# A preparation stage written as a straight plan: biases inside the products, rows normalised on ScalarE, rows of x loaded ahead of the weights, and results handed over by halves in the expert stage

## The chip, the cores and the metric

The kernel runs on one core of a Trainium2 chip. The core has five engines with their own instruction lists: TensorE (PE: products and transposes into PSUM), VectorE (DVE), ScalarE (ACT: functions from tables), GpSimd (POOL) and SyncE (SP), which here only issues DMAs. They run side by side and meet at semaphores. The metric is the time of one execution on the device in microseconds (us).

## The reference

The input x is (8, 1024, 256): 8 batches of 1024 rows of 256 channels. It goes through five blocks, each added to x: causal attention with 16 heads, a mixture of 8 experts (each row goes to one expert, at most 512 rows an expert), an RWKV-7 block, and the same mixture again. The change lies mostly in what is computed ahead of the recurrence of the RWKV-7 block. With xn the normalised rows:

```
shifted = rows of xn moved down by one, first row zero;  delta = shifted - xn
xr, xw, xk, xv, xa = xn + delta * x_r, x_w, x_k, x_v, x_a
r = xr @ W_r;  k = xk @ W_k;  v = xv @ W_v
log_w = -softplus(-(tanh(xw @ w_lora_a) @ w_lora_b + w_lora_bias)) - 0.5
a = sigmoid(xa @ a_lora_a @ a_lora_b + a_lora_bias)
g = sigmoid(r @ g_lora_a) @ g_lora_b + g_lora_bias
kk = k * k_k, scaled to norm 1 in each head;  k = k * (1 + (a - 1) * k_a)
o = recurrence over (r, log_w, k, v, -kk, kk * a);  bonus = ((r * k * r_k).sum(head)) * v
```

An expert computes `gelu(rows @ wi) @ wo`, scaled by the row's weight and added to the row.

## The kernel before, in words

Six stages follow one another with a barrier between: `attention`, `mixture`, `prepare`, `recurrence`, `finish`, `mixture`. The change touches `prepare` and the second half of `mixture`.

`prepare` works on one batch of 1024 rows a turn; all tensors lie in 8 tiles of 128 rows by 256 channels, or turned as 2 x 128 channels by 1024 rows. What is done in a turn, and in which order, stands in a list of jobs, `prepare_turn`, of stages with a half or a letter. Every engine goes through the same list and does its own part of each job, so an engine's instructions stand in the list's order, and each waits by semaphore for what it needs. A job marked `+` belongs to the next batch. The stages:

- `normalise` (L1997): VectorE makes mean and variance of each row (`bn_stats`, `bn_aggr`), ScalarE the root, VectorE the reciprocal and `xn`. `turn_x` (L1877, L1936): TensorE transposes `xn`, ScalarE copies it to `turned`.
- `mix` (L1979): VectorE makes `delta` (with the mix of r) and then the mixed rows of one letter, two instructions of 128x1024. v uses w's buffer, k uses a's.
- `r`, `k`, `v` (L1882): products with the full weights. ScalarE copies r to `r_rows`; `turn_r` transposes r (L1889).
- `w_inner`, `a_inner`, `g_inner` (L1896): the inner products with 64, 64 and 128 columns, then tanh, copy or sigmoid on ScalarE. `w`, `a`, `g` (L1909): the outer products. For w and a VectorE adds the bias into `z_w`, `z_a` (L2029), and ScalarE takes the sigmoid in place (L1957, L1960). For g VectorE adds the bias into `gate_sb` (L2034).
- `v` on ScalarE (L1940): three copies each half, into the packed rows that the recurrence reads.
- `key` (L2036): a chain on VectorE with two short steps on ScalarE, for each half of k. `bonus` (L2062): two VectorE instructions a half. GpSimd multiplies r by r_k and by k beside it (L1847, L1853).

Each product goes into one of four PSUM slots, handed out in the list's order; TensorE waits until the slot's last reader has emptied it. The turns of batches 0 to 6 are a hardware loop (`Fori`, L1770), the last turn is written out. Ahead of the first turn stands `prepare_start`. SyncE issues 20 loads of weights, then x of batches 0 and 1 (L1793, L1824); TensorE and VectorE wait for all of the weights at their start.

In the expert half of `mixture` (L1110 to L1273) TensorE makes the four tiles of an expert's result (`ps_res`, two PSUM banks) in one run and signals at its end; VectorE adds all four (L1221), signals, and GpSimd scatters four times (L1181).

## Time and profile before

| | us |
|---|---|
| median of three runs (lowest, highest) | 4567.62 (4563.92, 4568.98) |
| the profiled execution | 4533.91 |
| its span | 4532.2 |
| TensorE, VectorE, ScalarE, GpSimd busy | 3957.9, 3275.1, 1467.1, 2043.5 |
| mean granted TensorE clock | 0.929 |

The profile describes one execution. Times of rows count from the span's start. A row of a timeline has the start, the time busy, the engine, the line of the kernel, the operation, what is written and read, and the count of like instructions merged; in brackets stands how long the engine had stood idle before and which instruction ended the wait. PEclk and clock are the clock that TensorE was granted, as a share of 2.4 GHz, so 0.50 is 1.2 GHz. A float32 product is listed as two passes, so 16 products have a count of 32. Merged rows overlap their neighbours by a little; spacing is read from start to start.

### The profile page before, as it was taken

Reading aid. Unit: us, or ns where it says so; the run is one execution under the profiler, and the core shown is the slowest. Engines: PE = TensorE matmul, PEld = TensorE weight load, DVE = VectorE, ACT = ScalarE, POOL = GpSimd, SP = SyncE. Lnnn points to the kernel's source line nnn. Section 1 sums busy time; section 2 is a strip of 40 time slices with the busy share of each in tenths; the row PEclk is TensorE's granted clock in tenths of the full one; section 3 lists DMA queues with packets and bytes.
Section 4 is the critical chain, followed back from the end, with each engine's and each line's share of the span. In section 5 each row is a group of like instructions: output and inputs, shape, how many; then the busy total and the mean of one; then the engine's idle time right before and its main releaser. Section 6 shows DMA issues by size and latency. Waiting matters only on the chain. (4 is left out here: it accounts for less than half of the span.)

```text
span 4532.2 us, 66896 instructions
## 1 busy us (share of the span) xinstructions
PE 3957.9 (87%) x23448; PEld 2705.1 (60%) x23448; DVE 3275.1 (72%) x8604; ACT 1467.1 (32%) x2404; POOL 2043.5 (45%) x1669
## 2 busy tenths in 40 slices
PE   5999999999986895888669999999999999555698
PEld 2344444444436563666558888888888888444565
DVE  5777777877746002898769999999999999686410
ACT  2666666666665111444301111111111111013411
POOL 2211211221125221111168888888888888421522
PEclk7999999999996897999889999999999999776699
DMA  4322332332337231344443232323232322365432
GB/s 109 84 76 76 85 85 67 88 88 66 84 86 222 85 129 47 137 162 150 161 80 41 34 42 33 42 34 42 34 42 35 40 37 32 85 213 172 153 126 78
DMA packets 495631, 394.81 MB, mean 87 GB/s; under 512 B 298635, under 2 KB 457638, under 8 KB 489185
## 3 DMA queue, kind: packets, MB, share of 16 engines
q1 hardware_dynamic: 483040, 365.68, 32.8%
q0 software_dynamic: 12288, 25.28, 1.7%
q8 instruction: 168, 2.75, 0.3%
q14 instruction: 135, 1.10, 0.1%
HBM read 230.52 MB, written 167.97 MB: 88 GB/s over the span
## 5 line engine op out<-in xcount | busy, mean ns | idle before, releaser
L749 DVE TENSOR_REDUCE at_neg_max<-at_slot 128x1 f32<-128x512 f32 (+3 forms) x1216 | 745.8, 655 | 247.9 <-PE at_slot L541 245.1
L671 ACT ACTIVATE at_prob<-at_slot 128x512 f32<-128x512 f32 (+1 forms) x1216 | 631.1, 577 | 354.4 <-PE at_slot L561 353.5
L1613 PE MATMUL sc_added<-sc_outer,sc_ident 128*128 128x128 f32 x4096 | 586.4, 287 | 72.3 <-POOL sc_outer L1449 56.9
L1580 ACT ACTIVATE sc_seen<-sc_state 128x512 f32<-128x512 f32 x256 | 152.8, 597 | 1479.2 <-DVE sc_decayed L1529 1455.8
L1613 PEld LDWEIGHTS sc_added<-sc_outer,sc_ident 128*128 128x128 f32 x4096 | 496.9, 192 | 202.7 <-DVE sc_state L1561 109.8
L1462 POOL TENSOR_TENSOR sc_terms<-sc_seen,sc_pack 128x1024 f32<-128x1024 f32 (+2 forms) x288 | 604.9, 2142 | 13.8 <-PE sc_ps_o L1635 13.8
L1635 PE MATMUL sc_ps_o<-sc_terms,sc_ident 128*128 128x256 f32 x2048 | 607.6, 381 | 2.1 <-POOL sc_terms L1462 2.1
L389 POOL TENSOR_SCALAR_AFFINE_SELECT at_prob<-at_prob 128x512 f32<-128x512 f32 x256 | 162.8, 636 | 887.4 <-ACT at_prob L671 887.2
L541 PE MATMUL at_slot<-at_k_stack,at_q_stack 96*128 96x512 bf16 (+3 forms) x1536 | 458.7, 334 | 24.4 <-DMA at_k_stack<-parts 22.0
L1449 POOL TENSOR_TENSOR sc_outer<-sc_pack 128x2048 f32<-128x2048 f32 x128 | 467.2, 3672 | 5.0
L561 PE MATMUL at_slot<-at_q_stack,at_k_stack 99*128 99x512 bf16 (+3 forms) x1536 | 453.3, 331 | 12.1 <-ACT at_prob L671 11.7
L1525 DVE TENSOR_TENSOR sc_prod<-sc_state,sc_pack 128x256 f32<-128x256 f32 x1024 | 387.0, 424 | 3.7 <-POOL sc_from_v L1442 3.7
L1534 DVE TENSOR_REDUCE sc_u<-sc_prod 128x16 f32<-128x256 f32 x1024 | 386.5, 424 | 0.0
L1619 PE MATMUL sc_added<-sc_decayed,sc_ident 128*128 128x128 f32 x2048 | 365.1, 301 | 10.3 <-DVE sc_decayed L1529 1.0
L578 PE MATMUL at_values<-at_prob,at_v_rows 128*32 128x512 f32 (+3 forms) x3072 | 333.7, 505 | 16.2 <-POOL at_prob L389 16.2
L561 PEld LDWEIGHTS at_slot<-at_q_stack,at_k_stack 99*128 99x128 bf16 x1536 | 140.3, 97 | 325.9 <-issue 252.8
L1619 PEld LDWEIGHTS sc_added<-sc_decayed,sc_ident 128*128 128x128 f32 x2048 | 267.5, 190 | 103.3 <-DVE sc_decayed L1529 101.8
L1561 DVE TENSOR_TENSOR sc_state<-sc_added,sc_rank 128x128 f32<-128x128 f32 x1024 | 255.1, 295 | 92.8 <-PE sc_added L1624 65.5
L1635 PEld LDWEIGHTS sc_ps_o<-sc_terms,sc_ident 128*128 128x128 f32 x2048 | 313.5, 192 | 4.0 <-POOL sc_terms L1462 2.5
L1624 PE MATMUL sc_added<-sc_rank,sc_ident 128*128 128x128 f32 x2048 | 313.6, 276 | 2.2
L1624 PEld LDWEIGHTS sc_added<-sc_rank,sc_ident 128*128 128x128 f32 x2048 | 275.7, 191 | 55.1 <-DVE sc_rank L1539 5.1
L1539 DVE TENSOR_TENSOR sc_rank<-sc_u,sc_pack 128x128 f32<-128x128 f32 x1024 | 245.4, 281 | 0.0
(244 smaller groups left out, 6185.6 us busy)
## 6 DMA issues: line engine op xcount, KB each, us to landing
packed<-pr_pack SPq DMA_DIRECT2D x16, 3072.0 KB, 13.4
sc_pack<-packed SPq DMA_DIRECT2D x512, 96.0 KB, 3.6
parts<-at_parts SPq DMA_DIRECT2D x96, 256.0 KB
f_up_w<-in_ffn_wi SPq DMA_DIRECT2D x16, 1024.0 KB, 5.0
f_down_w<-in_ffn_wo SPq DMA_DIRECT2D x16, 1024.0 KB, 8.3
at_q_stack<-parts SPq DMA_DIRECT2D x32, 384.0 KB
at_k_stack<-parts SPq DMA_DIRECT2D x32, 384.0 KB
slots<-at_no_row SPq DMA_DIRECT2D x2, 4128.0 KB, 21.3
```

The source lines that it names most:

```text
L541: last = pe.matmul(by_head[:, j, :], q_stack[0:6 * D, h + j, qt * P:(qt + 1) * P], k_stack[0:6 * D, h + j, k0:k0 + tiles * P], start=not d ...
L561: last = pe.matmul(by_head[:, j, :], k_stack[0:6 * D + 3, h + j, kt * P:(kt + 1) * P], q_stack[0:6 * D + 3, h + j, q0:q1], start=True, sto ...
L671: act.activation(prob[:, first:first + n, q1 - tiles * P:q1], ps[:, 0:n * tiles * P].rearrange("p (n k) -> p n k", n=n), ACT.Exp)\
L749: dve.tensor_reduce(neg_max[:, chunk, qt, h:h + n], ps[:, 0:n * tiles * P].rearrange("p (n k) -> p n k", n=n), AX.X, ALU.max, negate=True) ...
L1449: own.up(pool.tensor_tensor(outer[m % 2][:, t, :].rearrange("p t (i j) -> p t i j", j=D), pack[m % 4][:, t, FV * D:(FV + 1) * D].unsqueeze ...
L1462: return pool.tensor_tensor(terms[m % 2][:].rearrange("p (n s) (j i) -> p n s i j", s=2, j=D)[:, pair:pair + n, step], seen[:, slot:slot + ...
L1525: dve.tensor_tensor(prod[:, h * STATE:(h + 1) * STATE].rearrange("p (s i j) -> p s i j", s=2, j=D), old[:, rows[h], :].unsqueeze(1).broadc ...
L1534: dve.tensor_reduce(u[:, pair, :, rows[h]], prod[:, h * STATE:(h + 1) * STATE].rearrange("p (s i j) -> p s i j", s=2, j=D), AX.X, ALU.add) ...
L1613: pe.matmul(added[h][:, 0:HALF], ident[:], outer[m % 2][:, 2 * n + s, h * HALF:(h + 1) * HALF], start=(s == 0), stop=False)
L1619: pe.matmul(added[h][:, 0:HALF], ident[:], decayed[:, h * HALF:(h + 1) * HALF], start=False, stop=False)
L1624: pe.matmul(added[h][:, 0:HALF], ident[:], rank[:, 0, h * HALF:(h + 1) * HALF], start=False, stop=True)\
L1635: last = pe.matmul(ps_o[m % 2][:], ident[:], by_column[:, n], start=first, stop=last_one)
```

## The change

In the list of a turn, `w_inner` stands ahead of `turn_r`; `normalise` is split into `stats` and `affine`, which stand behind `a` and around the mix of k, where `normalise` stood ahead of w; and `v` stands ahead of the next batch's `turn_x`. In `affine` VectorE makes the reciprocal and a shift, and ScalarE makes the normalised rows. The biases of w and a become a 65th row of their outer products' weights, against a row of ones in `w_inner` and `a_inner`; the sigmoids read PSUM directly, and their slots are now emptied by ScalarE. The loop over batches is written out. x of batch 0 is loaded ahead of the weights, and the wait for the weights stands behind `prepare_start` on TensorE and ahead of the first mix on VectorE. In the mixture the semaphores of the result count halves. The diff, cut to its core:

```diff
@@ -1215,14 +1217,16 @@
                     for k in range(2):
                         if not (last_turn and k):
                             take_cols(turn * 2 + k + 1, 1 - k)
-                        dve.wait_ge(res_made[k], 1 + turn + 1)
                         dve.wait_ge(fetched[k], (turn + 1) * OF_EXPERT)
                         for s in range(ST):
+                            if s % 2 == 0:
+                                dve.wait_ge(res_made[k], 1 + turn * 2 + s // 2 + 1)
                             last = dve.scalar_tensor_tensor(
                                 out=result[k][:, s, :], in0=ps_res[:, s * C:(s + 1) * C],
                                 scalar=rows[k][:, s, WEIGHT_COL:WEIGHT_COL + 1], in1=result[k][:, s, :],
                                 op0=ALU.mult, op1=ALU.add)
-                        last.then_inc(res_ready, 1)
+                            if s % 2:
+                                last.then_inc(res_ready, 1)
 
                 take_cols(0, 0)
...
@@ -1260,12 +1264,14 @@
                         if not (last_turn and k):
                             turn_rows(e + 1, turn + k, 1 - k)
                         pe.wait_ge(hid_ready, 1 + (e + 1) * (HC // 2))
-                        pe.wait_ge(res_ready, 1 + e)
                         for s in range(ST):
+                            if s % 2 == 0:
+                                pe.wait_ge(res_ready, RES_FIRST + e * 2 - 1 + s // 2)
                             for m in range(HC):
                                 last = pe.matmul(ps_res[:, s * C:(s + 1) * C], hidden[k][:, m, s * P:(s + 1) * P],
                                                  down_w[k][:, m, :], start=(m == 0), stop=(m == HC - 1))
-                        last.then_inc(res_made[k], 1)
+                            if s % 2:
+                                last.then_inc(res_made[k], 1)
 
                 turn_rows(0, 0, 0)
...
-PREPARE_USER = {"turn_x": "act", "r": "act", "turn_r": "act", "w_inner": "act", "g_inner": "act", "w": "dve",
-                "a_inner": "act", "g": "dve", "a": "dve", "v": "act", "k": "dve"}
+PREPARE_USER = {"turn_x": "act", "r": "act", "turn_r": "act", "w_inner": "act", "g_inner": "act", "w": "act",
+                "a_inner": "act", "g": "dve", "a": "act", "v": "act", "k": "dve"}
...
 
-    return [("normalise", 0), ("turn_x", 0), ("turn_x", 1), ("mix", "r"), ("mix", "w")]
+    return [("stats", 0), ("affine", 0), ("turn_x", 0), ("turn_x", 1), ("mix", "r"), ("mix", "w")]
 
...
     plus = lambda jobs: [("+" + stage, what) for stage, what in jobs] if ahead else []
-    return (halves("r") + halves("turn_r") + [("w_inner", 0), ("g_inner", 0), ("mix", "a")]
-            + plus([("normalise", 0)]) + halves("w") + [("mix", "v"), ("a_inner", 0)] + halves("g") + halves("a") + [("mix", "k")]
-            + plus(halves("turn_x")) + halves("v") + plus([("mix", "r")]) + halves("k")
-            + halves("key") + plus([("mix", "w")]) + halves("bonus"))
+    return (halves("r") + [("w_inner", 0)] + halves("turn_r") + [("mix", "a"), ("g_inner", 0)]
+            + halves("w") + [("mix", "v"), ("a_inner", 0)] + halves("g") + halves("a") + plus([("stats", 0)])
+            + [("mix", "k")] + plus([("affine", 0)]) + halves("v") + plus(halves("turn_x")) + plus([("mix", "r")])
+            + halves("k") + halves("key") + plus([("mix", "w")]) + halves("bonus"))
 
...
-        inner_b = {"w": sb("w_inner_b", [RW, C]), "a": sb("a_inner_b", [RW, C]), "g": sb("g_inner_b", [RG, C])}
-        wide = {m: sb("wide_" + m, [P, C]) for m in ("k_k", "k_a", "r_k", "w", "a", "g")}
+        inner_b = {"w": sb("w_inner_b", [RW + 1, C]), "a": sb("a_inner_b", [RW + 1, C]), "g": sb("g_inner_b", [RG, C])}
+        wide = {m: sb("wide_" + m, [P, C]) for m in ("k_k", "k_a", "r_k", "g")}
...
         rstd = sb("rstd", [P, TILES])
...
-            with eng.Fori(0, BATCH - 1) as b:
+            for b in range(BATCH - 1):
...
-            loads += [(inner_b[m][:], src) for m, src in (("w", w_b), ("a", a_b), ("g", g_b))]
+            loads += [(inner_b["w"][0:RW, :], w_b), (inner_b["a"][0:RW, :], a_b), (inner_b["g"][:], g_b)]
+            loads += [(inner_b["w"][RW:RW + 1, :], spread(w_bias, 1)), (inner_b["a"][RW:RW + 1, :], spread(a_bias, 1))]
             loads += [(wide[m][:], spread(src)) for m, src in
-                      (("k_k", k_k), ("k_a", k_a), ("r_k", r_k), ("w", w_bias), ("a", a_bias), ("g", g_bias))]
+                      (("k_k", k_k), ("k_a", k_a), ("r_k", r_k), ("g", g_bias))]
...
 
             load_x(0)
+            for dst, src in loads:
+                sp.dma_start(dst, src).then_inc(loaded, 16)
             load_x(1)
...
+            own.done()
+            for m in "wa":
...
         @block.tensor
         def _(pe):
-            pe.wait_ge(consts, 1 + 3)
...
         @block.scalar
         def _(act):
...
                         slots.wait_filled(act, s, use)
-                    if stage == "normalise":
+                    if stage == "stats":
                         act.wait_ge(var_ready, 1 + f + 1)
                         act.activation(std[:], mean_var[:, :, 1], ACT.Sqrt).then_inc(std_ready, 1)
+                    elif stage == "affine":
+                        act.wait_ge(affine_ready, 1 + f + 1)
+                        for n in range(TILES):
+                            act.activation(xn[:, n, :], x[:, n, :], ACT.Identity, bias=shift[:, n:n + 1],
+                                           scale=rstd[:, n:n + 1]).then_inc(xn_ready, 1)
                     elif stage == "turn_x":
                         if what == 0:
...
                         act.wait_ge(pack_stored[what], 1 + b * 16)
-                        act.wait_ge(z_used, 1 + b * 4 + what + 1)
+                        slots.wait_read(act, ("w", what))
...
-                        act.activation(inner[m][:], ps[0:width, :],
+                        act.activation(inner[m][0:width, :], ps[0:width, :],
                                        {"w": ACT.Tanh, "a": ACT.Copy, "g": ACT.Sigmoid}[m]).then_inc(emptied[s], 1)
                     elif stage == "w":
-                        slots.wait_read(act, (stage, what))
-                        act.activation(z["w"][what][:], z["w"][what][:], ACT.Sigmoid).then_inc(z_used, 1)
+                        act.wait_ge(w_packed, 1 + b * 2)
+                        act.activation(z["w"][what][:], ps[:], ACT.Sigmoid).then_inc(emptied[s], 1)
                     elif stage == "a":
-                        slots.wait_read(act, (stage, what))
-                        act.activation(a_sig[what][:], a_sig[what][:], ACT.Sigmoid).then_inc(z_used, 1)
+                        if b:
+                            act.wait_ge(chain, 1 + (b - 1) * TURN + 5 * (what + 1))
+                        act.activation(a_sig[what][:], ps[:], ACT.Sigmoid).then_inc(emptied[s], 1)
...
         def _(dve):
-            dve.wait_ge(consts, 1 + 3)
-            dve.wait_ge(loaded, 1 + 16 * N_LOADS)
...
                     mark = full_stage[:-len(stage)]
-                    if stage == "normalise":
+                    if stage == "stats":
...
                         dve.tensor_scalar(mean_var[:, :, 1], mean_var[:, :, 1], LN_EPS, None, ALU.add)\
                            .then_inc(var_ready, 1)
+                    elif stage == "affine":
                         dve.wait_ge(std_ready, 1 + f + 1)
+                        dve.wait_ge(xn_ready, 1 + f * TILES)
                         in_start.link(dve.reciprocal(rstd[:], std[:]))
-                        for t in range(TILES):
-                            dve.tensor_scalar(xn[:, t, :], x[:, t, :], mean_var[:, t, 0:1], rstd[:, t:t + 1],
-                                              ALU.subtract, ALU.mult).then_inc(xn_ready, 1)
+                        dve.scalar_tensor_tensor(out=shift[:], in0=rstd[:], scalar=-1.0, in1=mean_var[:, :, 0],
+                                                 op0=ALU.mult, op1=ALU.mult).then_inc(affine_ready, 1)
                     elif stage == "mix":
                         if what == "r":
...
                                                               turned[:, k, 1:T + 1], ALU.subtract))
                             in_start.done()
                             assert in_start.n == START
+                            if b is None:
+                                dve.wait_ge(loaded, 1 + 16 * N_LOADS)
                         mix(slots, what)
-                    elif stage in ("w", "a"):
-                        slots.wait_filled(dve, s, use)
-
-                        if stage == "w":
-                            dve.wait_ge(w_packed, 1 + b * 2)
-                        else:
-                            dve.wait_ge(z_used, 1 + b * 4)
-                        dve.tensor_tensor(by_tile(z[stage][what][:]), by_tile(slot[s][:]), wide_of[stage], ALU.add)\
-                           .then_inc(emptied[s], 1)
                     elif stage == "g":
```

TensorE, body of the turns of `prepare`, before (names: `pr_r_rows` is r ahead of its transposes, `pr_mixed_w` the mixed rows of w):

```order
L1894 MATMUL pr_slot<-pr_ident,pr_r_rows 128x128 x8
L249 ISA
L1894 MATMUL pr_slot<-pr_ident,pr_r_rows 128x128 x8
L1906 MATMUL pr_slot<-pr_mixed_w,pr_w_inner_a 64x512 x4
L262 REGISTER_ALU
L1906 MATMUL pr_slot<-pr_r_turned,pr_g_inner_a 128x512 x4
L262 REGISTER_ALU
L1914 MATMUL pr_slot<-pr_w_inner_b,pr_w_inner 128x256 x8
L1906 MATMUL pr_slot<-pr_mixed_a,pr_a_inner_a 64x512 x4
L1914 MATMUL pr_slot<-pr_g_inner_b,pr_g_inner 128x256 x8
```

The transposes of r stand first here, then the inner products of w and of the gate.

TensorE, the like place after:

```order
L1899 MATMUL pr_slot<-pr_big_r,pr_mixed_r 128x256 x16
L1918 MATMUL pr_slot<-pr_mixed_w,pr_w_inner_a 64x512 x4
L1906 MATMUL pr_slot<-pr_ident,pr_r_rows 128x128 x16
L1918 MATMUL pr_slot<-pr_r_turned,pr_g_inner_a 128x512 x4
L1926 MATMUL pr_slot<-pr_w_inner_b,pr_w_inner 128x256 x8
L1918 MATMUL pr_slot<-pr_mixed_a,pr_a_inner_a 64x512 x4
L1926 MATMUL pr_slot<-pr_g_inner_b,pr_g_inner 128x256 x8
L1926 MATMUL pr_slot<-pr_a_inner_b,pr_a_inner 128x256 x8
L1899 MATMUL pr_slot<-pr_big_v,pr_mixed_w 128x256 x16
L1893 MATMUL pr_slot<-pr_ident,pr_xn 128x128 x16
L1899 MATMUL pr_slot<-pr_big_k,pr_mixed_a 128x256 x16
```

The inner product of w has moved ahead of the transposes of r, and v ahead of the transposes of the next batch's `pr_xn`.

VectorE, the same turns, before, from the aggregates of the next batch to w:

```order
L2004 BN_AGGR pr_mean_var<-pr_stats 128x2 x8
L43 REGISTER_ALU
L2006 TENSOR_SCALAR pr_mean_var<-pr_mean_var 128x8
L2008 REGISTER_ALU
L2009 RECIPROCAL pr_rstd<-pr_std 128x8
L43 REGISTER_ALU
L2011 TENSOR_SCALAR pr_xn<-pr_x,pr_mean_var,pr_rstd 128x256 x8
L2026 ISA
L2029 TENSOR_TENSOR pr_z_w<-pr_slot,pr_wide_w 128x1024
L252 ISA
L2029 TENSOR_TENSOR pr_z_w<-pr_slot,pr_wide_w 128x1024
L252 REGISTER_ALU
```

The statistics and the normalising stand directly ahead of w's bias; the gate's addition (L2034) follows three rows below.

VectorE after, from the mix of a to the mix of r:

```order
L2004 SCALAR_TENSOR_TENSOR pr_mixed_a<-pr_delta,pr_mu_a,pr_turned 128x1024 x2
L2004 SCALAR_TENSOR_TENSOR pr_mixed_w<-pr_delta,pr_mu_v,pr_turned 128x1024 x2
L2046 TENSOR_TENSOR pr_gate_sb<-pr_slot,pr_wide_g 128x1024 x2
L2018 BN_STATS pr_stats<-pr_x 128x6 x8
L2022 BN_AGGR pr_mean_var<-pr_stats 128x2 x8
L2024 TENSOR_SCALAR pr_mean_var<-pr_mean_var 128x8
L2004 SCALAR_TENSOR_TENSOR pr_mixed_a<-pr_delta,pr_mu_k,pr_turned 128x1024 x2
L2029 RECIPROCAL pr_rstd<-pr_std 128x8
L2030 SCALAR_TENSOR_TENSOR pr_shift<-pr_rstd,pr_mean_var 128x8
L2036 TENSOR_TENSOR pr_delta<-pr_turned 128x1024 x2
L2004 SCALAR_TENSOR_TENSOR pr_mixed_r<-pr_delta,pr_mu_r,pr_turned 128x1024 x2
```

The statistics stand behind the gate's addition, and both additions into `pr_z_w` and `pr_z_a` and the eight normalising instructions are gone.

ScalarE, the same turns, before, from the turned rows on:

```order
L1936 ACTIVATE pr_turned<-pr_slot 128x1024 x2
L252 REGISTER_ALU
L1941 ISA
L1944 ACTIVATE pr_pack<-pr_z_w 128x64x16
L1946 ACTIVATE pr_pack<-pr_r_rows 128x64x16
L1947 ACTIVATE pr_pack<-pr_slot 128x64x16
L252 REGISTER_ALU
L1944 ACTIVATE pr_pack<-pr_z_w 128x64x16
L1946 ACTIVATE pr_pack<-pr_r_rows 128x64x16
L1947 ACTIVATE pr_pack<-pr_slot 128x64x16
```

The turned rows come first, then three copies for each half.

ScalarE after:

```order
L1946 ACTIVATE pr_std<-pr_mean_var 128x8
L1950 ACTIVATE pr_xn<-pr_x,pr_shift,pr_rstd 128x256 x8
L1963 ACTIVATE pr_pack<-pr_z_w 128x64x16
L1965 ACTIVATE pr_pack<-pr_r_rows 128x64x16
L1966 ACTIVATE pr_pack<-pr_slot 128x64x16
L1963 ACTIVATE pr_pack<-pr_z_w 128x64x16
L1965 ACTIVATE pr_pack<-pr_r_rows 128x64x16
L1966 ACTIVATE pr_pack<-pr_slot 128x64x16
L1955 ACTIVATE pr_turned<-pr_slot 128x1024 x2
```

The two copies that fill `pr_turned` have moved from ahead of the six copies into `pr_pack` to behind them, and eight instructions that write `pr_xn` stand ahead of both.

## Rows read from the trace of the kernel before

**Rows 1.** timeline, VectorE (start, us, engine, line, operation, count, [idle]): keys, turns 0, 6, 7.
```profile
1831.19 1.23 DVE L2041 SCALAR_TENSOR_TENSOR pr_scaled<-pr_z_a,pr_wide_k_a 128x1024 f32<-128x1024 f32 x1 [1.69 <-PE pr_slot L1887]
...
2181.64 1.23 DVE L2041 SCALAR_TENSOR_TENSOR pr_scaled<-pr_z_a,pr_wide_k_a 128x1024 f32<-128x1024 f32 x1 [1.69 <-PE pr_slot L1887]
...
2236.69 1.23 DVE L2041 SCALAR_TENSOR_TENSOR pr_scaled<-pr_z_a,pr_wide_k_a 128x1024 f32<-128x1024 f32 x1 [6.95 <-PE pr_slot L1887]
```

**Rows 2.** busy us by window: PE, PEld, DVE, ACT, POOL; PEclk, DMA share, GB/s.
```profile
1949.10:2006.40 57.30, 49.90 (x201) 35.91 (x200) 51.92 (x64) 28.09 (x29) 11.31 (x4) 0.91 0.44 165
1964.00:1972.00 8.00, 5.45 (x19) 3.86 (x20) 7.83 (x8) 4.88 (x5) 0.38 (x1) 0.50 0.00 0
```

**Rows 3.** VectorE's timeline through one turn.
```profile
1942.53 2.36 DVE L2017 TENSOR_TENSOR pr_delta<-pr_turned 128x1024 f32<-128x1024 f32 x2 [2.08 <-ACT pr_turned L1936]
1944.92 2.48 DVE L1986 SCALAR_TENSOR_TENSOR pr_mixed_r<-pr_delta,pr_mu_r,pr_turned 128x1024 f32<-128x1024 f32 x2
1949.10 1.23 DVE L2041 SCALAR_TENSOR_TENSOR pr_scaled<-pr_z_a,pr_wide_k_a 128x1024 f32<-128x1024 f32 x1 [1.69 <-PE pr_slot L1887]
...
1967.57 2.48 DVE L1986 SCALAR_TENSOR_TENSOR pr_mixed_w<-pr_delta,pr_mu_w,pr_turned 128x1024 f32<-128x1024 f32 x2
...
1979.23 2.70 DVE L2000 BATCH_NORM_STATS2 pr_stats<-pr_x 128x6 f32<-128x256 f32 x8
...
1983.39 2.67 DVE L2011 TENSOR_SCALAR pr_xn<-pr_x,pr_mean_var,pr_rstd 128x256 f32<-128x256 f32 x8
1985.98 2.35 DVE L2029 TENSOR_TENSOR pr_z_w<-pr_slot,pr_wide_w 128x1024 f32<-128x1024 f32 x2
```

**Rows 4.** TensorE's timeline through the same turn.
```profile
1945.44 7.07 PE L1887 MATMUL pr_slot<-pr_big_k,pr_mixed_a 128*128 128x256 f32 x32
...
1965.69 3.65 PE L1894 MATMUL pr_slot<-pr_ident,pr_r_rows 128*128 128x128 f32 x16 [6.28 <-ACT pr_r_rows L1939]
1970.20 5.41 PE L1906 MATMUL pr_slot<-pr_mixed_w,pr_w_inner_a 128*64 128x512 f32 x8 [0.85 <-DVE pr_mixed_w L1986]
1975.54 3.70 PE L1906 MATMUL pr_slot<-pr_r_turned,pr_g_inner_a 128*128 128x512 f32 x8
...
1986.39 3.72 PE L1914 MATMUL pr_slot<-pr_g_inner_b,pr_g_inner 128*128 128x256 f32 x16
```

**Rows 5.** ScalarE's timeline of the same turn: copies of w, turned halves.
```profile
1942.33 1.06 ACT L1944 ACTIVATE pr_pack<-pr_z_w 128x1024 f32<-128x1024 f32 x1
...
1945.64 1.06 ACT L1944 ACTIVATE pr_pack<-pr_z_w 128x1024 f32<-128x1024 f32 x1 [0.40 <-PE pr_slot L1887]
...
1997.78 1.94 ACT L1936 ACTIVATE pr_turned<-pr_slot 128x1024 f32<-128x1024 f32 x2 [1.33 <-DVE pr_mixed_a L1986]
```

**Rows 6.** ScalarE's timeline in the first mixture's routing.
```profile
1387.85 1.28 ACT L994 ACT_TABLE_LOAD   x1
1389.14 0.21 ACT L994 ACTIVATE f_std<-f_roots 128x16 f32<-128x16 f32 x1
1390.74 4.04 ACT L999 ACTIVATE f_base<-f_x,f_shift,f_base_scale 128x256 f32<-128x256 f32 x8 [1.39 <-DVE f_shift L1036]
```

**Rows 7.** timeline of prepare's start; last, x's landing from its tile's view.
```profile
1746.96 0.38 SPq L1794 DMA_DIRECT2D pr_big_r<-in_attn_b_W_r  x1
...
1757.30 17.34 SPq L1800 DMA_DIRECT2D pr_x<-x_mixed  x2
1765.98 2.71 DVE L2000 BATCH_NORM_STATS2 pr_stats<-pr_x 128x6 f32<-128x256 f32 x8 [35.55 <-DMA pr_x<-x_mixed]
...
1784.16 9.78 PE L1887 MATMUL pr_slot<-pr_big_r,pr_mixed_r 128*128 128x256 f32 x32 [6.19 <-DVE pr_mixed_r L1986]
...
DMA to landing us min/median/max: 5.5/6.6/8.2
```

**Rows 8.** timeline of the first mixture's tail.
```profile
1728.77 1.66 DVE L1221 SCALAR_TENSOR_TENSOR f_result<-f_ps_res,f_rows,f_result 128x256 f32<-128x256 f32 x4 [27.27 <-PE f_ps_res L1266]
...
1735.05 0.97 POOL L1181 DMA_INDIRECT x_mixed<-f_result,f_rows  x1 [0.30 <-issue]
```

## What I expect, before seeing the result

> **What bounds the kernel now.** I read the table of 40 slices first, then the busy times by stage, then each engine's timeline through one turn of the preparation, then the waits at the stage's edges. The program is a row of stages, and the change touches two: `prepare` (about 1736 to 2280 us) and the expert halves of the two mixtures. Everything else keeps its time.
>
> In `prepare` one turn works on one batch. I date a turn by K, the start of the first key instruction on VectorE. K stands at 1831.19 for turn 0, at 2181.64 for turn 6, at 2236.69 for turn 7 [rows 1]: six periods in 350.45 us, 58.4 each. A plain turn (K = 1949.10 to 2006.40) takes 57.3 with VectorE busy 51.9 and TensorE 49.9 [rows 2]. VectorE's list sets that pace: it goes from one instruction to the next and stops only 2.08 us for the turned rows and 1.69 for the first product of k [rows 3]. TensorE has one long stop, 6.28 us before the transposes of r; after it the granted clock is 0.50 (1.2 GHz) from 1964 to 1972, where the turn's mean is 0.91 [rows 2, 4].
>
> In the experts TensorE is the pace, and only the tail stands open: VectorE starts on the last products at 1728.77, its four operations take 1.66, and the last of four scatters leaves at 1735.05, 4.6 behind VectorE's end [rows 8].
>
> **What is taken off VectorE.** Eight normalising operations, 2.6 us by starts (1983.39 to 1985.98), the pair that adds w's bias, 2.3 [rows 3], the like pair for a, 2.3; an operation of 128x8 is added, 0.2 by the reciprocal that lies between statistics and normalising. So its list falls by 7.0 us: if it still set the pace, a turn would take 50.3. TensorE's products keep their number and shape but for a 65th row, priced at nothing, since 64 and 128 rows take the same time here (3.6 us a stage [rows 4]). ScalarE gets eight operations of 128x256 in `Identity`, 4.04 us by the same form in the mixture [rows 6]; it is busy 28.1 of 57.3 [rows 2], so as work they fit.
>
> **What is moved, and what that makes.** Three things now lie in one row. (1) The inner product of w stands ahead of r's transposes. It needs the mix of w, which VectorE makes behind both keys, at K + 18.5 to 21. Before, the transposes ran in that time; now TensorE stands still from the end of r's products to the mix, some 14 us. (2) The statistics of the next batch stand behind the gate's addition instead of ahead of w. (3) On ScalarE the six copies of v, w and r stand ahead of the two that turn the next batch's rows; before, they stood behind. So the way from one K to the next is a closed path, all from the rows:
> - K to the inner product of w: 21.1 (1970.20 less 1949.10) [rows 3, 4].
> - That product: 3.6 at 2.4 GHz (as the gate's, 3.70 with its drain), 7.3 at 1.2 GHz. The row shows 5.41 with a stop of 6.28 and the slow transposes ahead. With 14 us of standing still and no slow work ahead of it I take 6.3.
> - Transposes of r, 1.9 (twice that at 1.2 GHz), ScalarE's copy of the second, 1.1.
> - Gate's inner product, w, inner product of a: 10.85 (1975.54 to 1986.39). Then g's products 3.65 and the second addition 1.2 (half of such a pair) [rows 3, 4]: VectorE gets free at K + 46.15. Its mixes of a and v were done near K + 33, so it waits about 11 us for g, and statistics are queued behind that wait.
> - Statistics and the short operations up to the normalising, 4.2 (1979.23 to 1983.39); the mix of k between them, 2.4 as that of w [rows 3].
> - ScalarE: eight normalisings 4.04 with handing over 0.1; six copies 5.8 (three of them from 1942.33 to 1945.64 less the wait of 0.40, twice); two turned halves 1.95 [rows 5, 6].
> - VectorE: differences and mix of r, 4.9 (1942.53 to 1947.40), with handing over 4.95 [rows 3].
>
> Sum: 21.1 + 6.3 + 1.9 + 1.1 + 10.85 + 4.9 + 4.2 + 2.4 + 4.15 + 5.8 + 1.95 + 4.95 = 69.6. Beside it lie TensorE's a (3.65), v (6.9), transposes and k: k's first half fills at about K + 63.5, before VectorE asks for it at 69.6. Six periods: 6 x (69.6 - 58.4) = +67.2.
>
> Turn 0 has no keys ahead and its mix of w is ready early. Before: 47.0 from r's first product (1784.16) to K. After: r 9.8 (it starts at 1.2 GHz, as in the row), 3.65, then the same path from the transposes on, 42.2: 55.65, so +8.6 [rows 1, 7]. Turn 7 has nothing of a next batch: K of turn 6 to K of turn 7 was 55.05; after it is 30.4 up to the gate's inner product, 10.85, g and a 7.3, v 6.9, half of k 3.45: 58.9, so +3.9.
>
> **The start.** The rows of x were issued 10.34 us behind the first weight (1746.96, 1757.30) and VectorE began at 1765.98, 8.7 later [rows 7]. Now x goes first, with nothing ahead of it in its queue: I take 6.4 for its landing, between the 5.5 of the quickest load of x [rows 7] and 8.7, so the statistics come 12.6 earlier. ScalarE's normalising is 1.6 longer than VectorE's, leaving -11.0. The weights issue during the statistics and land about 10 us behind x, before the first mix needs them (from the first statistics to r's first product lie 18.2 us now [rows 7]); if that cover failed it would cost the few us by which they are late. Two one-row memsets on GpSimd, each below the 1.81 of the 128x2050 one, run while x flies.
>
> **The experts.** The first two scatters leave while TensorE makes the second half. Saved at the tail: two VectorE operations (0.83) and two of four scatters (at 1.28 each, 2.56), 3.4 us, twice [rows 8]. In the steady turns TensorE has no wait on results to lose; the added wait, ahead of the second half, is for an addition made long before: 0, and if it did bind it would be at most 0.8 for each of 16 experts.
>
> **Unrolled loops.** I price them at nothing: the only stops of VectorE in a turn are the two named, so the loop's edge has no gap to give back beyond their 3.8 us, and what straight code may cost in fetching is bounded above by no row; I leave it to the range.
>
> Sum: -3.4 - 11.0 + 8.6 + 67.2 + 3.9 - 3.4 = +61.9. The profiled execution took 4533.9, which gives 4595.8; the runs' median, 4567.6, lies 34 above it, so the time comes out near **4629.5**.
>
> The Trainium skill (ScalarE: Activation LUTs, What ACT_TABLE_LOAD costs) puts 1.28 us of load and 1.38 of drain on each change of table. The rows show the load and the next activation 0.01 behind it (1387.85 + 1.28, 1389.14) [rows 6], so no drain. By the row the root is there when VectorE asks at K + 52.2; by the page it would come about 0.3 late, some 2 us over seven turns, and the time would be 4631.5.
>
> **Rivals.**
> - *VectorE's list stays the bound.* For: it sets the pace now and loses 7.0 of 57.3. Then seven turns give 49 less than before, last turn 3, edges 17.8: 4567.6 - 70 = 4498. It decides as soon as the path above is under 57.3 us; so 12.3 us of it would have to be false, that is, the transposes, w, or the statistics would have to stand elsewhere than the program writes them. Against: every engine keeps its own order. 9 in 100.
> - *Path and gains meet near zero.* The path at about 60 us (the wait for g covered by half), so that +10 in the turns meets the edges' -18 and turn 0's +8: 4568. 4 in 100.
> - *The clock makes it worse.* The six periods before sum to 6.6 us more than six plain ones, so this happens now. After 14 us of standing still, and with short stops ahead of the gate's product and of the next transposes, low clock may last through transposes (+1.9) and return inside g or a (+3.3): 74 a turn, +26 more, 4656. For: each longer stop in the rows is followed by 1.2 GHz; against: it came back after about 8 us there, and in turn 0 after 5.4 (r took 9.8 for 7.07 at full clock [rows 4, 7]). 12 in 100.
> - *The forecast*, w's product between 3.6 and 7.3: 66.9 to 71.5 a turn, 4613 to 4645. 75 in 100.
>
> **Numbers.** A change of 0.2% is what can be told here. Slower: 0.87; within 0.2%: 0.04; faster: 0.09. The range goes from 4606 (the low end, and x or the scatters a little better) to 4656, the clock's case.
>
> **What would show it.** Right: K every 69 to 71 us; VectorE waiting 10 to 12 us for g's products and 9 to 11 for the turned rows; TensorE still for about 14 us ahead of w's inner product; ScalarE's eight normalisings, then six copies, then the turned halves; VectorE's first statistics near 1750; the last scatters at 3.4 less behind the last product. Wrong: w's inner product starting before K + 20, statistics ahead of g, or a period under 66.

## The result and the profile after

The changed kernel takes 4619.9 us (median of four runs, 4616.06 to 4622.67) against 4565.8 for the kernel before (4556.76 to 4568.98): ratio 1.0121, 95% interval 1.0104 to 1.0139, 54 us slower. On a second chip, where the kernel before takes 4531.6, it was 4583.3, ratio 1.0117 (1.0101 to 1.0134), 52 slower. The forecast was 4629.5, 62 slower.

Its page shows less work on VectorE and as much on TensorE as before, in a longer span:

```profile
span 4618.3 us, 66332 instructions
...
PE 3960.0 (86%) x23448; PEld 2700.7 (58%) x23448; DVE 3232.0 (70%) x8516; ACT 1478.7 (32%) x2454; POOL 2042.6 (44%) x1671
...
PEclk7999999999985998889879999999999999876599
```

VectorE's timeline through a turn (K = 1913.69 to 1981.97), with the lines that answer to [rows 1, 3]:

```profile
1913.69 1.22 DVE L2053 SCALAR_TENSOR_TENSOR pr_scaled<-pr_z_a,pr_wide_k_a 128x1024 f32<-128x1024 f32 x1
...
1931.89 2.48 DVE L2004 SCALAR_TENSOR_TENSOR pr_mixed_w<-pr_delta,pr_mu_w,pr_turned 128x1024 f32<-128x1024 f32 x2
...
1943.58 4.56 DVE L2004 SCALAR_TENSOR_TENSOR pr_mixed_w<-pr_delta,pr_mu_v,pr_turned 128x1024 f32<-128x1024 f32 x2
1956.36 1.22 DVE L2046 TENSOR_TENSOR pr_gate_sb<-pr_slot,pr_wide_g 128x1024 f32<-128x1024 f32 x1 [8.22 <-PE pr_slot L1926]
1958.09 1.23 DVE L2046 TENSOR_TENSOR pr_gate_sb<-pr_slot,pr_wide_g 128x1024 f32<-128x1024 f32 x1 [0.50 <-PE pr_slot L1926]
1959.23 2.70 DVE L2018 BATCH_NORM_STATS2 pr_stats<-pr_x 128x6 f32<-128x256 f32 x8
...
1962.79 2.47 DVE L2004 SCALAR_TENSOR_TENSOR pr_mixed_a<-pr_delta,pr_mu_k,pr_turned 128x1024 f32<-128x1024 f32 x2
...
1965.41 0.17 DVE L2030 SCALAR_TENSOR_TENSOR pr_shift<-pr_rstd,pr_mean_var 128x8 f32<-128x8 f32 x1
1977.17 2.36 DVE L2036 TENSOR_TENSOR pr_delta<-pr_turned 128x1024 f32<-128x1024 f32 x2 [11.59 <-ACT pr_turned L1955]
1979.57 2.48 DVE L2004 SCALAR_TENSOR_TENSOR pr_mixed_r<-pr_delta,pr_mu_r,pr_turned 128x1024 f32<-128x1024 f32 x2
1981.97 1.22 DVE L2053 SCALAR_TENSOR_TENSOR pr_scaled<-pr_z_a,pr_wide_k_a 128x1024 f32<-128x1024 f32 x1
```

It waits 8.22 us for the first half of the gate's product and 11.59 for the turned rows; statistics start only behind the gate. TensorE in the same turn, for [rows 4]:

```profile
1913.92 7.14 PE L1899 MATMUL pr_slot<-pr_big_r,pr_mixed_r 128*128 128x256 f32 x32 [2.52 <-DVE pr_mixed_r L2004]
1934.52 6.04 PE L1918 MATMUL pr_slot<-pr_mixed_w,pr_w_inner_a 128*64 128x512 f32 x8 [13.46 <-DVE pr_mixed_w L2004]
1940.48 1.96 PE L1906 MATMUL pr_slot<-pr_ident,pr_r_rows 128*128 128x128 f32 x16
1943.70 3.67 PE L1918 MATMUL pr_slot<-pr_r_turned,pr_g_inner_a 128*128 128x512 f32 x8 [1.25 <-ACT pr_r_turned L1968]
...
1954.33 3.72 PE L1926 MATMUL pr_slot<-pr_g_inner_b,pr_g_inner 128*128 128x256 f32 x16
1957.89 3.62 PE L1926 MATMUL pr_slot<-pr_a_inner_b,pr_a_inner 65*128 65x256 f32 x16
1961.34 7.07 PE L1899 MATMUL pr_slot<-pr_big_v,pr_mixed_w 128*128 128x256 f32 x32
1969.80 1.94 PE L1893 MATMUL pr_slot<-pr_ident,pr_xn 128*128 128x128 f32 x16 [1.38 <-ACT pr_xn L1950]
1972.51 7.17 PE L1899 MATMUL pr_slot<-pr_big_k,pr_mixed_a 128*128 128x256 f32 x32 [0.77 <-ACT pr_pack L1966]
```

It stands still for 13.46 us ahead of w's inner product, which then takes 6.04 us where 3.65 is its time at full clock. ScalarE, for [rows 5]:

```profile
1962.59 1.28 ACT L1946 ACT_TABLE_LOAD   x1
1963.88 0.21 ACT L1946 ACTIVATE pr_std<-pr_mean_var 128x8 f32<-128x8 f32 x1
1965.61 4.04 ACT L1950 ACTIVATE pr_xn<-pr_x,pr_shift,pr_rstd 128x256 f32<-128x256 f32 x8 [1.52 <-DVE pr_shift L2030]
1969.56 1.04 ACT L1963 ACTIVATE pr_pack<-pr_z_w 128x1024 f32<-128x1024 f32 x1
...
1972.36 1.04 ACT L1963 ACTIVATE pr_pack<-pr_z_w 128x1024 f32<-128x1024 f32 x1
...
1975.15 1.92 ACT L1955 ACTIVATE pr_turned<-pr_slot 128x1024 f32<-128x1024 f32 x2
```

Eight normalisings, six copies, and only then the two turned halves for which VectorE waits. The table load ends at 1963.87 (1962.59 + 1.28) and the root begins at 1963.88, as in [rows 6].

Busy times of the turn, for [rows 2] (columns as there): nobody is busy for more than 49 of 68.28 us.

```profile
1913.69:1981.97 68.28, 48.91 (x200) 34.57 (x200) 46.77 (x55) 29.06 (x35) 11.28 (x4) 0.90 0.37 139
```

The start, for [rows 7]: x is issued first, and VectorE begins 6.3 us behind.

```profile
1764.42 0.38 SPq L1808 DMA_DIRECT2D pr_x<-x_mixed  x1
...
1770.74 2.71 DVE L2018 BATCH_NORM_STATS2 pr_stats<-pr_x 128x6 f32<-128x256 f32 x8 [20.36 <-DMA pr_x<-x_mixed]
...
1790.48 9.89 PE L1899 MATMUL pr_slot<-pr_big_r,pr_mixed_r 128*128 128x256 f32 x32 [6.19 <-DVE pr_mixed_r L2004]
```

### The profile page after: what moved, and what is told of

Its sections match the earlier page's. It is cut to its first block and busy times, and to the rows that moved or that the text cites. A ratio compares the mean times of both kernels' runs of the same rounds, so it can differ in the third digit from the quotient of the medians.

```text
span 4618.3 us, 66332 instructions
## 1 busy us (share of the span) xinstructions
PE 3960.0 (86%) x23448; PEld 2700.7 (58%) x23448; DVE 3232.0 (70%) x8516; ACT 1478.7 (32%) x2454; POOL 2042.6 (44%) x1671
```

## Experiments

Each kernel ran beside the kernel before on the same chip. K of each turn is read as in [rows 1], from the first key instruction; "six turns" are the periods from turn 0 to turn 6.

| kernel | against before (us) | ratio, 95% | a turn (us) | turn 7 |
|---|---|---|---|---|
| before, profiled | | | 57.3, twice 60.6 | 55.05 |
| changed | +54.1 | 1.0121 (1.0104 to 1.0139) | 68.2 to 68.4 | 58.20 |
| `moves_alone` | +50.6 | 1.0114 (1.0099 to 1.0130) | 64.9 to 65.0 | 58.17 |
| `turn_r_first` | +28.1 | 1.0064 (1.0049 to 1.0080) | 64.6 to 64.9, once 62.7 | 54.78 |
| `turn_x_first` | +61.1 | 1.0135 (1.0119 to 1.0150) | 69.0 to 71.2 | 58.70 |
| `only_experts` | -6.8 | 0.9983 (0.9974 to 0.9992) | 57.3 to 57.5, twice 60.6 | 53.47 |
| `old_order` | -9.2 | 0.9982 (0.9971 to 0.9993) | 58.4 to 58.6, twice 59.8 to 60.0 | 54.48 |
| `mix_w_early` | +8.9 | 1.0018 (1.0008 to 1.0028) | 61.5 to 63.0 | 49.79 |
| `short_path` | -66.3 | 0.9851 (0.9835 to 0.9868) | 51.1, once 51.9 | 49.35 |
| `before_unrolled` | +0.8 | 0.9999 (0.9989 to 1.0008) | 57.1, twice 60.4 to 60.7 | 55.49 |
| `short_order_before` | -9.5 | 0.9980 (0.9971 to 0.9990) | 55.7 (three), 58.4 (three) | 50.94 |
| `changed_again` | +51.7 | 1.0117 (1.0101 to 1.0134) | 68.2 to 68.4 | 58.20 |

**The order alone.** On the kernel before:

```diff
-    return (halves("r") + halves("turn_r") + [("w_inner", 0), ("g_inner", 0), ("mix", "a")]
-            + plus([("normalise", 0)]) + halves("w") + [("mix", "v"), ("a_inner", 0)] + halves("g") + halves("a") + [("mix", "k")]
-            + plus(halves("turn_x")) + halves("v") + plus([("mix", "r")]) + halves("k")
+    return (halves("r") + [("w_inner", 0)] + halves("turn_r") + [("mix", "a"), ("g_inner", 0)]
+            + halves("w") + [("mix", "v"), ("a_inner", 0)] + halves("g") + halves("a") + plus([("normalise", 0)])
+            + [("mix", "k")] + halves("v") + plus(halves("turn_x")) + plus([("mix", "r")]) + halves("k")
```

> The kernel before with only its list of a turn put in the new order (w_inner ahead of turn_r, normalise behind a, v ahead of turn_x); biases, sigmoids and normalising stay on VectorE as before, the loop stays, no load moves. If the order makes the closed path: VectorE waits for w's product made late, statistics behind it, turned rows behind the copies, and a turn takes about 65 us against 58.4; six turns +40, turn 0 +5, turn 7 +3, so about 48 us slower than before (4613). If the loss came from the work given to ScalarE (eight normalisings, sigmoids from PSUM) and not from the order, this stays within 5 us of before.

Measured: 4615.3, 50.6 slower, 64.9 a turn. The order by itself slows the kernel: of the 59.2 us that the changed kernel loses in six turns, it makes 38.9 (389.37 against 350.45). The other 20, 3.4 a turn, come with the rest of the change, in this order. VectorE has a's additions less and starts the statistics 3.1 us sooner behind K (45.5 instead of 48.7), but from the first of them to the first of the six copies it is 10.3 us instead of 3.8: the mix of k and ScalarE's normalising (4.0) now lie between. That the totals are so near, +50.6 and +54.1, is chance: the 20 us are nearly what the changed kernel saves at its edges (17.7).

**One move undone at a time.** In the changed kernel, `turn_r` ahead again:

```diff
-    return (halves("r") + [("w_inner", 0)] + halves("turn_r") + [("mix", "a"), ("g_inner", 0)]
+    return (halves("r") + halves("turn_r") + [("w_inner", 0)] + [("mix", "a"), ("g_inner", 0)]
```

> The changed kernel with one move undone: the transposes of r stand ahead of w's inner product again. If the path is as worked out, the transposes run while the mix of w is still being made and the gate's inner product starts 3.8 us sooner behind K (26.2 instead of 30.0): six turns and turn 7 at 3.8 each, turn 0 one us longer, so 25 us less than the changed kernel (about 4595), a turn 64.5 us. If this move costs nothing because v, turned rows or ScalarE set the end alone: no change against the changed kernel (4620).

Measured: 4592.9, 28.1 over the kernel before where the changed kernel is 54.1 over it, so 26 back (25 expected); a turn of 64.7 (64.5 expected). The transposes are a term of the path. Its trace also has something that the changed kernel's has not: behind the short stop ahead of r the clock falls to 0.50 in all turns but the first, and r takes 8.83 us for 7.14. The one turn of 62.7 is the one in which it does not fall there.

```profile
1969.35 8.83 PE L1899 MATMUL pr_slot<-pr_big_r,pr_mixed_r 128*128 128x256 f32 x32 [2.51 <-DVE pr_mixed_r L2004]
```

Then `turn_x` ahead of v:

```diff
-            + [("mix", "k")] + plus([("affine", 0)]) + halves("v") + plus(halves("turn_x")) + plus([("mix", "r")])
+            + [("mix", "k")] + plus([("affine", 0)]) + plus(halves("turn_x")) + halves("v") + plus([("mix", "r")])
```

> The changed kernel with one move undone: the next batch's transposes and turned copies stand ahead of v again. ScalarE then hands over the turned rows 5.8 us sooner. But TensorE now stands still from the end of a (K + 47.7) to the normalised rows (K + 56.1), and v (6.9) and half of k (3.45) come behind the transposes, so k's first half is filled at K + 68.4, as late as VectorE asked before: my working gives a turn of 68.4 us and no change (4620). If instead the six copies were simply a term of the path, it would be 5.8 x 7 = 41 us less (4579).

Measured: 4625.9, 61.1 over the kernel before (the changed kernel: 54.1); no gain, as expected, and a turn is 0.6 to 2.8 us longer than the working. TensorE's timeline and the clock show what the working left out:

```profile
2024.25 3.62 PE L1926 MATMUL pr_slot<-pr_a_inner_b,pr_a_inner 65*128 65x256 f32 x16
2036.29 3.65 PE L1893 MATMUL pr_slot<-pr_ident,pr_xn 128*128 128x128 f32 x16 [8.42 <-ACT pr_xn L1950]
2039.73 7.45 PE L1899 MATMUL pr_slot<-pr_big_v,pr_mixed_w 128*128 128x256 f32 x32
2047.01 5.34 PE L1899 MATMUL pr_slot<-pr_big_k,pr_mixed_a 128*128 128x256 f32 x24
```

TensorE stood still for 8.42 us for the normalised rows, and the transposes ran at half speed (3.65 for 1.9) and v's first products too. In the changed kernel the six copies lie on the path by its timeline (VectorE waits 11.59 us for the turned rows behind them). This run cannot show their price, since taking them off hands the end to TensorE's v and k at once. What undoing this third move (the copies of v ahead of the turned rows) gives once the statistics stand early again, with `w_inner` left ahead, no run tried.

**All three undone.** The list of the kernel before, with `stats` and `affine` where `normalise` stood:

```diff
+    return (halves("r") + halves("turn_r") + [("w_inner", 0), ("g_inner", 0), ("mix", "a")]
+            + plus([("stats", 0), ("affine", 0)]) + halves("w") + [("mix", "v"), ("a_inner", 0)] + halves("g") + halves("a") + [("mix", "k")]
+            + plus(halves("turn_x")) + halves("v") + plus([("mix", "r")]) + halves("k")
+            + halves("key") + plus([("mix", "w")]) + halves("bonus"))
```

> The changed kernel with all three moves undone: the order of the kernel before, with stats and affine side by side where normalise stood; everything else of the change stays (biases in the products, sigmoids from PSUM, normalising on ScalarE, straight loop, x first, halves in the experts). Path worked out: gate's inner product at K + 26.2, but ScalarE normalises (to K + 38.3) and loads a table (1.3) ahead of w's sigmoids, so w's slots come free at K + 40.6, g's second half and a wait for it, a ends at 46.2, then transposes, v and half of k: a turn of 58.5 us. Edges as in the changed kernel: -11 at the start, -6.8 at the tails. So about 4548, 17 us less than before, although VectorE has 7 us less to do a turn. If VectorE's list were the bound in this order too, a turn of about 51 to 52 us and some 4505.

Measured: 4523.7 against 4532.9, 9.2 less (17 expected), a turn of 58.4 and twice 60. The traces' terms, read as in the table further down, give 14.5 less: edges -17.8, turn 0 +0.7, six turns +3.2, turn 7 -0.6. The profiled execution, at 4519.0, agrees with them (13.9 less); what lies between it and the median stays open. TensorE waits in the middle of g for a slot that ScalarE empties late, because the normalising and a table load stand ahead of w's sigmoids:

```profile
1972.86 1.99 PE L1926 MATMUL pr_slot<-pr_g_inner_b,pr_g_inner 128*128 128x256 f32 x8
1976.66 1.99 PE L1926 MATMUL pr_slot<-pr_g_inner_b,pr_g_inner 128*128 128x256 f32 x8 [1.81 <-ACT pr_z_w L1976]
```

```profile
1970.23 4.04 ACT L1950 ACTIVATE pr_xn<-pr_x,pr_shift,pr_rstd 128x256 f32<-128x256 f32 x8 [0.47 <-DVE pr_shift L2030]
1974.29 1.28 ACT L1976 ACT_TABLE_LOAD   x1
1975.58 1.94 ACT L1976 ACTIVATE pr_z_w<-pr_slot 128x1024 f32<-128x1024 f32 x2
```

So even in the old order VectorE's 7 us were not to be had: VectorE waits for the first key (4.28 us here, 1.69 before), and the path through ScalarE and the slots takes the gain. What is left are the edges.

**The mix of w ahead of the keys.** In the changed kernel:

```diff
-            + [("mix", "k")] + plus([("affine", 0)]) + halves("v") + plus(halves("turn_x")) + plus([("mix", "r")])
-            + halves("k") + halves("key") + plus([("mix", "w")]) + halves("bonus"))
+            + [("mix", "k")] + plus([("affine", 0)]) + halves("v") + plus(halves("turn_x")) + plus([("mix", "r"), ("mix", "w")])
+            + halves("k") + halves("key") + halves("bonus"))
```

> The changed kernel with one job moved: the mix of w of the next batch stands right behind that of r, ahead of the keys, instead of behind both keys. If the wait for that mix is a term of the path, w's inner product starts when the second half of k has left its slot (K + 12.6) instead of K + 20.8, the gate's inner product at about K + 21.6 instead of 30.0; the mix adds its 2.4 ahead of K: a turn of about 63 us against 68.3, turn 7 8 us shorter, together 38 us less than the changed kernel, about 4582. If the wait of 13.5 us is only a symptom and something later sets the end: no change (4620).

Measured: 4541.9, 8.9 over before, where the changed kernel is 51.7 over it on another chip, on which before takes nearly the same time (4531.6): 43 us back (38 expected), by moving two instructions a turn. The turn is 61.5, not 63. The wait ahead of w's inner product has changed its releaser from the mix to VectorE's last reading of k's second half, which frees the slot:

```profile
1964.68 5.07 PE L1918 MATMUL pr_slot<-pr_mixed_w,pr_w_inner_a 128*64 128x512 f32 x8 [5.38 <-DVE pr_pack L2061]
1969.68 1.97 PE L1906 MATMUL pr_slot<-pr_ident,pr_r_rows 128*128 128x128 f32 x16
```

**A list that shortens the path.** In the changed kernel:

```diff
+    return (halves("r") + [("w_inner", 0)] + halves("turn_r") + [("g_inner", 0)]
+            + halves("w") + [("mix", "a")] + plus([("stats", 0)]) + [("a_inner", 0)] + plus([("affine", 0)])
+            + [("mix", "v")] + halves("g") + halves("a") + [("mix", "k")] + plus(halves("turn_x")) + halves("v")
+            + plus([("mix", "r"), ("mix", "w")]) + halves("k") + halves("key") + halves("bonus"))
```

> The changed kernel with another list: mix of w behind that of r; mix of a, then statistics, ahead of a_inner; affine behind a_inner; the next batch's transposes ahead of v. Worked out with the same rows: w_inner K + 12.6 to 17.5, gate's inner product 20.6 to 24.2, w 27.8, a_inner 31.4, g 35.0, a 38.6, transposes 40.5, v 47.4, half of k 50.9: a turn of 51 us, TensorE the bound (46 us of products, 5 of standing still). Six turns at 51 instead of 58.4, turn 7 at 49 instead of 55, start -11, tails -6.8: about 4497, 68 us less than before. If the long turns came from the work on ScalarE and not from the order, the turn stays over 60 us here.

Measured: 4466.7 against 4532.9, ratio 0.9851 (0.9835 to 0.9868), 66 us less than before; 51.1 a turn as worked out. It beats both kernels with the changed kernel's work, instruction for instruction but for two table loads more a turn on ScalarE (14 in all, 1.28 us each). TensorE is busy 47.5 of 51.1, VectorE 44.8:

```profile
1920.14:1971.24 51.10, 47.52 (x201) 34.55 (x200) 44.84 (x53) 31.67 (x37) 11.28 (x4) 0.97 0.50 186
```

```profile
1932.80 5.34 PE L1918 MATMUL pr_slot<-pr_mixed_w,pr_w_inner_a 128*64 128x512 f32 x8 [2.33 <-DVE pr_pack L2061]
1938.07 1.96 PE L1906 MATMUL pr_slot<-pr_ident,pr_r_rows 128*128 128x128 f32 x16
1941.28 3.67 PE L1918 MATMUL pr_slot<-pr_r_turned,pr_g_inner_a 128*128 128x512 f32 x8 [1.25 <-ACT pr_r_turned L1968]
```

Its two long stops are the slot of k's second half (2.33) and the turned r (1.25). Behind the first the clock falls to 0.50 (1934 to 1937.5), and w's inner product takes 5.34 us for 3.65.

**The same order without the lighter VectorE.** The kernel before with such a list:

```diff
+    return (halves("r") + [("w_inner", 0)] + halves("turn_r") + [("g_inner", 0), ("mix", "a")]
+            + plus([("normalise", 0)]) + halves("w") + [("a_inner", 0), ("mix", "v")] + halves("g") + halves("a")
+            + [("mix", "k")] + plus(halves("turn_x")) + halves("v")
+            + plus([("mix", "r"), ("mix", "w")]) + halves("k") + halves("key") + halves("bonus"))
```

> The kernel before with only its list of a turn in nearly the order of short_path (mix of w behind that of r, normalise behind the mix of a, then w, a_inner, the next batch's transposes ahead of v); all work stays on VectorE, the loop stays, no load moves, the expert stage as before. It parts what the order gives from what the lighter list of VectorE gives. Worked out: VectorE's list has 53 us to do in a turn, so a turn of 53 to 54 against 58.4, turn 7 5 us shorter, no edges: about 33 us less than before (ratio 0.9927). If the order alone were worth the whole gain of short_path it would be 56 us less (51.1 a turn); if the order needed the lighter list to give anything, no change.

Measured: 4522.1 against 4531.6, 9.5 less, not 33: I had priced VectorE's list and not the waits on it. The addition of w's bias holds w's slot and, through ScalarE, the inner product of a; TensorE stops twice for it, and the clock falls to 0.50: a's products take 5.27 us (3.7 at full clock) and the transposes 3.67 (for 1.9). The three turns of 58.4 are those in which it falls there; in the three of 55.7 it does not.

```profile
1980.42 1.99 PE L1914 MATMUL pr_slot<-pr_g_inner_b,pr_g_inner 128*128 128x256 f32 x8 [1.79 <-DVE pr_z_w L2029]
1983.54 5.27 PE L1914 MATMUL pr_slot<-pr_a_inner_b,pr_a_inner 64*128 64x256 f32 x16 [1.13 <-ACT pr_a_inner L1953]
1988.74 3.67 PE L1881 MATMUL pr_slot<-pr_ident,pr_xn 128*128 128x128 f32 x16
```

So of `short_path`'s 66 us some 10 go with the order on the old work and 18 with the edges (start 11.1 and two tails of 3.3, in the table below). The other 38 come only with both together: the changed kernel's work in the old order gave nothing in the turns, and is worth having once the order lets it. The split is rough, since the two short lists are not quite the same (the mixes of a and v, and the normalising, stand elsewhere), and no run parts the biases inside the products from the normalising on ScalarE.

**Edges and loop.** The kernel before with the mixture of the changed one (its diff stands above):

> The kernel before with only the halves of the expert stage. If the tail of each expert stage is all that this part touches: VectorE's last two additions end 0.8 us behind the last product and the last scatter 2.6 us sooner, so 3.4 us less twice, 6.8 us in all, ratio 0.9985; the turns of prepare stay at 57.3 to 60.6 us. If the added waits held TensorE in the steady turns it would be up to 13 us slower instead. It also shows whether the first mixture's routing, 18 us shorter in the profiled execution of the kernel before than in that of the changed one, is a property of the code ahead of it (then it is short here too) or of that one execution.

Measured: 6.8 less, as worked out (the interval allows 4 to 12). The traces show it free of that noise: from the last product to the first load of `prepare` 14.89 us against 18.24, and from the last product of all to the end 11.85 against 15.18, 6.7 together. The first mixture's routing was long here too. And the loop written out, here for the engines, and SyncE's in the same way:

```diff
-            with eng.Fori(0, BATCH - 1) as b:
+            for b in range(BATCH - 1):
```

> The kernel before with only the loop over batches of prepare written out on every engine. Priced at nothing in the prediction: 4565 within 5 us, turns of 57.3 us as with the loop. If the loop's edge or its register waits cost something, up to 3.8 us a turn (VectorE's stops) would go; if straight code costs fetching, it gets slower and the trace shows stops with no releaser at new places.

Measured: +0.8, ratio 0.9999 (0.9989 to 1.0008): nothing.

**The changed kernel again.**

> The changed kernel once more, with a second profile, beside runs of the kernel before on the same chip. If the 68.3 us turn is a closed path of fixed durations, each of the six periods is 68.2 to 68.4 again and the ratio lies within 1.010 to 1.014; the time as such may lie 30 us lower if the chip is one with the short routing.

Measured: 4583.3 against 4531.6; the periods 68.2 to 68.4 again.

## Why the prediction was right

Term by term, from the traces of before and after:

| term | forecast | measured | from |
|---|---|---|---|
| tail of the first mixture | -3.4 | -3.3 | last product's end to the first load: 18.24, then 14.96 |
| start | -11.0 | -11.1 | first load to r's first product: 37.20, then 26.06 |
| turn 0 | +8.6 | +7.9 | r's first product to K: 47.03, then 54.89 |
| six turns | +67.2 | +59.2 | 350.45, then 409.70 |
| turn 7 | +3.9 | +3.1 | K of turn 6 to K of turn 7: 55.05, then 58.20 |
| tail of the second mixture | -3.4 | -3.3 | last product's end to the end: 15.18, then 11.86 |
| sum | +61.9 | +52.5 | medians: +54.1 and +51.7 |

*The closed path.* Every link is there, within 0.35 us, by the timeline of after: K to w's inner product 20.8 (21.1 forecast), that product 6.0 (6.3), transposes and copy 3.2 (3.0), three stages 10.6 (10.85), g and its second addition 4.9 (4.9), statistics and mix of k up to the normalising 6.4 (6.6), normalising 3.95 (4.15), copies 5.6 (5.8), turned halves 2.0 (1.95), differences and mix 4.8 (4.95): 68.3 against 69.6. The excess of the forecast, 1.3 a turn and 8 in all, is many small roundings upward and 0.3 of the clock's price. `moves_alone` kept only the order, `turn_r_first` and `mix_w_early` each took one link away, and the turn moved by about what was worked out (64.9 for 65, 64.7 for 64.5; 61.5 for 63, 1.5 better than priced).

*The signs.* Three of those that I named as right were missed by a little, though the path held. K came every 68.2 to 68.4 us, not 69 to 71. VectorE waited 8.7 us for the gate's products, not 10 to 12: its mixes ended at K + 34.5 and not near 33, and g came 0.6 sooner behind K. It waited 11.59 for the turned rows, not 9 to 11; my own sum had 11.9 there (4.15 + 5.8 + 1.95), so that sign did not follow from it. The others held: 13.46 us ahead of w's inner product, the order on ScalarE, the last scatter 3.3 sooner behind the last product. The first statistics came 6.3 behind the issue of x, as priced, but at 1770.7 and not near 1750, since the first mixture's routing took 18.6 longer in this trace. No sign of being wrong came: w's inner product starts at K + 20.8. And the high end of the range for w's product was added up wrongly: 7.3 instead of 6.3 gives 70.6 a turn, not 71.5.

*The absolute time.* That 4619.9 lies between 4606 and 4656 rests on the chip as well: where `changed_again` ran, the same kernel took 4583.3, below that range. What the prediction can be held to is the difference, 62 against 52 to 54.

*VectorE's list as the bound* (the rival on the other side): refuted by every run with the changed kernel's work; in `short_path`, where the turn comes near the 50.3 of that rival, TensorE is busier than VectorE (47.5 against 44.8). In the changed kernel the mix of v took 4.56 us while GpSimd multiplied beside it, and not the 2.47 that it took before, where GpSimd stood still (the mix of a had GpSimd beside it in both, 4.57 and 4.60). I had not charged that; it lay inside the wait for g.

*ScalarE's part at nothing as work* held (29.1 busy of 68.3), and its place on the path was charged in full (normalising 3.95, copies 5.6, turned halves 2.0).

*The clock.* It fell to 0.50 inside the long stop (r's products ended at 1921.1; the clock is 1.00 up to 1924 and 0.50 from 1926), and was back when the transposes began (1.00 from 1940); it did not fall again inside g or a. The rival that made it worse did not come in the changed kernel; it did in `turn_x_first` and `short_order_before`. The kernel before had it too: its two turns of 60.6 are those in which a's products ran at 0.50.

*A drain behind a table load.* In the turns of `prepare` no trace has one, on either side of a load: the root's 1963.88 follows 1962.59 + 1.28, and in the rows of `old_order` above the load at 1974.29 stands right behind the normalising (1970.23 + 4.04) and the sigmoids 0.01 behind the load. The rule of the Trainium skill (ScalarE: Activation LUTs, What ACT_TABLE_LOAD costs), by which 2 us would have come on top, does not hold here.

*Median and profile of before.* The 34 us between them, which I left unexplained, lie mostly in the two routings. The first mixture's takes, from the start of the last store of attention to the first product of the experts, 142.6 to 143.4 us in the traces of before, `old_order`, `mix_w_early`, `short_path`, `before_unrolled`, `short_order_before` and `changed_again`, and 155.5 to 162.0 in those of `only_experts`, `moves_alone`, `turn_r_first`, `turn_x_first` and the changed kernel. The second's, from the last product ahead of it to its last gate product, takes 108 to 111 in the first seven and 122 to 125 in the other five. Its code is the same in all, and the changed kernel has one trace in either group (162.0 and 142.9, 122.6 and 108.1): 34 of the 37 us between its two traces. The groups go with the chip that the runs were taken on; whether it is the chip or something else that differed between those sets of runs was not looked into.

Not tried: x first alone, and the 65th row alone. Their terms rest on the traces (start -11.1; the outer products with 65 rows take 3.6 us as those with 64), not on a run of their own.

## What to carry to other kernels

In a plan that all engines follow in order, lay out one turn as a closed path, from an instruction to itself a turn later, before believing any engine's busy time: here VectorE was 91% busy (51.9 of 57.3) and lost 7 us of work, and the turn grew by 11. Three moves that look harmless together put waits ahead of work that others wait for; the same work in another order is 1.5% faster than before instead of 1.2% slower. And where a move is undone singly to find the culprit, ask what is next: `turn_x_first` gave nothing, though by the timeline its link was on the path.

## What the runs showed of the hardware

- The granted clock fell to 0.50 in or right behind each of the single stops of 5 us and more that were read (13.46 in the changed kernel, 8.42 in `turn_x_first`, 5.76 in `old_order`, 5.38 in `mix_w_early`). Short stops went either way. The stop of 2.52 ahead of r was followed by full pace in the changed kernel (7.14 us for r), and the like stop of 2.51 in `turn_r_first` by 0.50 in six of seven (8.83); a stop of 2.33 in `short_path` was followed by 0.50, and so were two stops close together, 1.79 and 1.13 in three turns of `short_order_before`, 0.67 and 1.13 in two turns of the kernel before.
- Outer products with 65 rows took 3.62 us for 16 instructions, those with 64 rows 3.72: the row that carries the bias cost nothing on TensorE.
- The time from one chip to another differed by 33 us of 4550 for the kernel before and by 37 for the changed one, and most of it in one kind of stage (the two routings, 19 and 14 us for the changed kernel); ratios agreed (1.0121 and 1.0117).
